# A state-space layer and a quantised feed-forward layer on eight cores: other buffers, queues and order for the weight preparation and the quantisation

## The chip, the cores and the metric

The kernel runs on one Trainium2 chip, on all 8 NeuronCores, with no exchange between them. Each core has a matrix engine (TensorE, PE in the profile), a vector engine (VectorE, DVE), an activation engine (ScalarE, ACT), a general engine (GpSimd, POOL) and a sync engine (SyncE, SP) that here only issues DMAs. The metric is the device time of the slowest core in microseconds (us); the kernel before takes 9439.07 us (median of 3 runs, 9436.37 to 9455.23).

## The reference

The input x is 2 sequences of 8192 tokens of 1024 features. Core c owns 2048 tokens of one sequence. What is computed, cut to its steps:

```python
# state-space half
xz = layernorm(layernorm(x)) @ W_in.T + b_in ; x_proj, z = split(xz) ; z = silu(z)
B_proj = x_proj @ W_B.T * dt.mean()
x_mean = causal convolution of B_proj with mean over d of A_bar[d] ** t
y = ((x_mean @ W_C.T + D_skip * x_proj) * z) @ W_out.T + b_out + residual
x = x + layernorm(y)
# feed-forward half (4096 hidden features)
def act_quant(x):    s = 127 / max|x| per token ; return clip(round(x * s), -128, 127) / s
def weight_quant(w): s = 1 / mean|w| ;            return clip(round(w * s), -1, 1) / s
h = act_quant(layernorm(x)) @ weight_quant(w1).T
h = silu(depthwise_conv1d(h, 3 taps) + conv_b)
x = x + layernorm(act_quant(h) @ weight_quant(w2).T)
```

## The kernel before

The program is written out by hand. `Pr` (from L49) keeps one list of instructions for each engine; an instruction is appended to its engine's list where the Python code calls it, with the semaphore values it has to wait for. So on each engine the order is that of the code, and an instruction that waits holds back all that is behind it on its engine. This is true of the DMAs too: `P.dma` appends the transfer to SP's list, or to POOL's with `eng="gpsimd"`. `P.bar()` gives the present value of every semaphore, and what waits for it waits for all work so far.

The stages of a core, one after the other:

1. A scan over the 6144 tokens ahead of its own, in three passes (L546). `range_pipeline` (L438) loads tiles of 128 tokens into `a_xtm`, transposes them and makes the sums for the layernorm.
2. Weight preparation (L618 to L650). Each of the 16 row blocks of W_in is loaded as 128x1024 (512 KB) into one of two halves of `a_big` (`natb`). For each of its 8 column blocks: PE transposes 128x128 into `ps0` or `ps1`, ACT writes the high bf16 part to `a_w1`, DVE writes the low part to `a_wr`, and a DMA stores this (32 KB) to `s_wlo` in DRAM. The next transpose waits for the store before it (`after=[lw] + wk[-2:]`, and a DMA's semaphore is waited for up to its latest value), so there are 128 such rounds. The 8 row blocks of W_out go the same way, without the store. Loads and stores are all on POOL's queue.
3. `range_pipeline` over the core's own tokens (L652, behind the barrier `ph4` ahead of stage 2), the projection (L683), the state-space part (L757 to L850).
4. The output projection in nine tiles of 256 tokens (L873), which ends with x2 in DRAM. Its tiles lie in `a_w1`'s memory, `a_st2`, `a_wr` and the last quarter of `a_big`.
5. `quant_weight` for w1 (L976): a first pass loads the 32 row blocks of w1 (SP's queue, two buffers in `a_xh`), ACT writes the absolute values to `a_xl`, DVE adds them up per row and into one column (three instructions one behind the other), then come the mean and its broadcast by way of DRAM; a second pass loads w1 again, rounds it to -1, 0, 1 and transposes it into `a_w1` and `a_w2`.
6. The feed-forward loop (L1130), 8 rounds `fi` of 256 tokens. The work of a round, in the order of the data:
   - x2 is loaded; squares (ACT) and column sums (PE); mean, maximum, scales, which go through rows in DRAM (`cols_to_row`, `bcast_read`);
   - the input is scaled and shifted: 16 POOL instructions of 128x258, four pairs ahead of the first `floor_sub` and four beside it (the list `uts2`), in `a_xh`. `floor_sub` (L255) is DVE's rounding, 17 instructions, and is called twice on 128x1032;
   - 32 hidden blocks of 128: 8 matmuls each, and DVE scales the sum from PSUM (`h_e`);
   - the convolution (ACT and DVE), silu (ACT), the maximum over the hidden features (DVE), scales, broadcast to `t_bt`;
   - the rounding of h, in 8 groups of 4 hidden blocks. For seven groups POOL multiplies (4 instructions of 128x256, two buffers in `a_xh`, function `emit_ug`) and DVE rounds: one instruction and a `floor_sub` of 128x1024. Group 7 is rounded by `floor_tri_act` (L280) in two halves: POOL multiplies (2 instructions), ACT does 18 absolute values of 128x512, DVE five instructions; the second half uses the same buffers and waits for the first. Each group is stored to `s_hq` from POOL's queue.

   This last step is put off by a round. `emit_hq_gps` (L1066), at the start of round fi+1, appends POOL's products for groups 0 and 1 and all of group 7; `emit_hq_vec` (L1095), behind the two input roundings of round fi+1, appends the DVE roundings of groups 0 to 6, the other products and the stores. After the last round both are called once more.
7. `quant_weight` for w2, and the output loop (L1310) of four tiles of 512 tokens, whose y tile changes between the two halves of `a_xl` (`yoff`).

## Time and profile before

| | |
|---|---|
| median of 3 timed runs | 9439.07 us |
| profiled execution, slowest core | 9412.07 us |
| span of that core (core 5) from first to last instruction | 9410.5 us |
| spans of the 8 cores | 9369.6 to 9410.5 us, granted clock 0.607 or 0.608 |
| PE, DVE, ACT, POOL busy in the span | 31%, 36%, 11%, 6% |
| DMA | 283.16 MB, mean 30 GB/s |
| chain that ended last, by what it spent time in | DVE 34%, PE 27%, DMA 15%, issue 11%, ACT 7%, POOL 1% |

Stage by stage, in us from the start of the span: scan 0 to 1693, weight preparation to 2381, own tokens, projection and state-space part to 3564, output projection to 4524, w1 to about 4970, feed-forward loop to 8332, w2 to about 8770, output to 9410. No engine is busy for even half of the span: in a program of this kind the time is a chain of waits from engine to engine, and a share of busy time says little. What counts is, in each stage, which instruction or transfer ends last before the next can start.

### The profile page before, as it was taken

What the parts mean: (1) busy time and instruction counts of PE and PEld (TensorE: products, weight loads), DVE (VectorE), ACT (ScalarE), POOL (GpSimd) and SP (SyncE); (2) the same over time, 40 slices, a digit from 0 to 9 for tenths busy, and PEclk for the clock granted to TensorE, in tenths of its full rate; (3) what the DMA queues carried; (4) which work ended last, traced back from release to release, by engine and by line L of the source; (5) the groups of instructions that cost most, each with busy time, mean ns of one, the idle gap of its engine ahead of it and who ended that gap; (6) DMA issues with size and microseconds to landing.
All of it is one profiled execution on the core that took longest, in us unless ns stands there. A gap on an engine that the chain in (4) does not pass through costs nothing.

```text
span 9410.5 us, 47615 instructions; the slowest of 8 cores (9369.6 to 9410.5 us)
## 1 busy us (share of the span) xinstructions
PE 2911.7 (31%) x12144; PEld 1440.0 (15%) x12144; DVE 3392.8 (36%) x6255; ACT 1064.5 (11%) x2053; POOL 520.5 (6%) x604
## 2 busy tenths in 40 slices
PE   3545354111557644333133010102101010103464
PEld 1121212000123343222011000101000000101121
DVE  0111110101112212333444575574757557564212
ACT  0111011001100020000101111202021120210000
POOL 0000000110000000000000111010111111000000
PEclk9955555555568856666556565656656565655686
DMA  1010101000001211111210000000000000021111
GB/s 32 26 41 32 42 27 38 28 23 25 31 32 40 37 39 26 32 36 32 90 45 17 8 9 8 14 10 11 9 8 9 8 14 10 3 98 54 42 56 59
DMA packets 170576, 283.16 MB, mean 30 GB/s; under 512 B 60305, under 2 KB 122987, under 8 KB 165893
## 3 DMA queue, kind: packets, MB, share of 16 engines
q1 hardware_dynamic: 157640, 246.56, 8.8%
q0 software_dynamic: 12672, 33.57, 1.2%
q8 instruction: 106, 1.74, 0.1%
q14 instruction: 158, 1.29, 0.0%
HBM read 223.21 MB, written 55.10 MB: 30 GB/s over the span
## 4 chain that ended last, share of the span: by engine, by line
DVE 34%; PE 27%; DMA 15%; issue 11%; ACT 7%; SPq 3%; DVEq 1%; POOL 1%; ACTq 0%; POOLq 0%
PE ps L243 21%; PE ps L246 6%; DVE a_xh_f L264 6%; DVE a_xh_f L260 5%; ACT a_st L272 4%; DMA a_st<-s_logat 3%; SPq L82 3%; DVE a_xh_f L252 3%; DMA s_wlo<-a_wr 2%; DVE a_st L264 2%; DMA s_rows<-t_tiny 2%; DVE a_w_f L252 2%; DVE a_w L249 2%; DVE a_xl_f L264 2%; DVE a_xtm L252 1%
## 5 line engine op out<-in xcount | busy, mean ns | idle before, releaser
L243 PE MATMUL ps<-a_xtm_b,a_w 128*128 128x258 bf16 x2048 | 295.8, 290 | 1548.1 <-DVE a_xh_f L252 1133.9
L264 DVE SCALAR_TENSOR_TENSOR a_xh_f<-a_xh_f 128x1024 f32<-128x1024 f32 x448 | 575.4, 1284 | 47.3 <-DVE a_xh_f L260 0.9
L243 PE MATMUL ps<-a_st,c_o1f 128*1 128x256 f32 (+3 forms) x992 | 415.0, 533 | 370.7 <-ACT a_st L272 323.8
L243 PE MATMUL ps<-a_xh,a_w 128*128 128x512 bf16 (+2 forms) x1664 | 386.1, 396 | 245.1 <-DMA a_xh<-s_hq 67.8
L246 PE MATMUL ps<-c_id,a_big 128*128 128x128 f32 x208 | 92.9, 447 | 1165.2 <-DVE a_big L252 532.4
L243 PEld LDWEIGHTS ps<-a_xtm_b,a_w 128*128 128x128 bf16 x2048 | 193.4, 102 | 1650.8 <-issue 1618.9
L246 PE MATMUL ps<-c_id,a_xh_f 128*128 128x128 f32 (+1 forms) x536 | 238.8, 445 | 658.9 <-DVE a_xh_f L252 392.3
L252 DVE TENSOR_TENSOR a_xl<-ps,a_xh 128x256 bf16<-128x256 f32 (+1 forms) x264 | 109.9, 416 | 857.5 <-ACT a_xh L272 857.5
L260 DVE TENSOR_SCALAR a_xh_f<-a_xh_f 128x1024 f32<-128x1024 f32 (+1 forms) x464 | 350.6, 756 | 144.3 <-POOL a_xh_f L252 95.2
L272 ACT ACTIVATE a_xl_f<-a_xh_f,c_cw 128x256 f32<-128x256 f32 x256 | 130.0, 508 | 1948.3 <-DVE a_xh_f L252 1948.3
L252 POOL TENSOR_TENSOR a_xh_f<-a_xl_f,t_bt 128x256 f32<-128x256 f32 x224 | 240.7, 1103 | 1950.4 <-DMA t_bt<-s_rows 1084.8
L243 PE MATMUL ps<-t_bt,a_st 128*128 128x16 f32 x1024 | 228.1, 373 | 322.9 <-ACT a_st L272 322.9
L249 DVE CAST a_w<-ps 128x128 bf16<-128x128 f32 x512 | 149.0, 291 | 359.3 <-PE ps L246 359.3
L243 PEld LDWEIGHTS ps<-t_bt,a_st 128*128 128x128 f32 x1024 | 223.1, 330 | 331.1 <-issue 331.1
L246 PE MATMUL ps<-c_id,a_xtm 128*128 128x128 f32 (+3 forms) x536 | 188.2, 441 | 244.8 <-DMA a_xtm<-xp 165.4
L243 PEld LDWEIGHTS ps<-a_xh,a_w 128*128 128x128 bf16 x1664 | 171.4, 105 | 459.3 <-issue 319.9
L264 DVE SCALAR_TENSOR_TENSOR a_xl_f<-a_xh_f,c_cw,a_xl_f 128x256 f32<-128x256 f32 x512 | 226.0, 481 | 27.1 <-DVE a_xl_f L264 0.5
L252 DVE TENSOR_TENSOR a_xh_f<-ps,a_xtm 128x258 f32<-128x258 f32 x256 | 109.0, 426 | 345.8 <-PE ps L243 345.8
L264 DVE SCALAR_TENSOR_TENSOR a_wr<-ps,c_vc,a_w 128x128 bf16<-128x128 f32 x128 | 44.8, 350 | 517.2 <-ACT a_w L272 517.2
L252 POOL TENSOR_TENSOR a_xh_f<-a_st,a_abc 128x258 f32<-128x258 f32 x64 | 54.4, 849 | 3175.4 <-DMA a_abc<-s_rows 3167.1
L246 PEld LDWEIGHTS ps<-c_id,a_big 128*128 128x128 f32 x208 | 37.9, 182 | 1220.0 <-issue 1220.0
L246 PEld LDWEIGHTS ps<-c_id,a_xh_f 128*128 128x128 f32 (+1 forms) x536 | 96.9, 181 | 800.4 <-issue 800.4
(189 smaller groups left out, 4883.0 us busy)
## 6 DMA issues: line engine op xcount, KB each, us to landing
a_st<-s_logat SPq DMA_DIRECT2D x64, 512.0 KB, 4.0
a_xh_f<-w SPq DMA_DIRECT2D x64, 512.0 KB, 3.8
a_xh_f<-w SPq DMA_DIRECT2D x16, 2048.0 KB, 8.2
a_xtm<-xp SPq DMA_DIRECT2D x48, 512.0 KB, 4.8
s_hq<-a_big_b POOLq DMA_DIRECT2D x64, 256.0 KB, 3.3
a_xh<-s_hq SPq DMA_DIRECT2D x128, 128.0 KB, 3.5
a_st<-s_x SPq DMA_DIRECT2D x64, 129.0 KB, 3.2
a_xtm<-xo SPq DMA_DIRECT2D x16, 512.0 KB, 4.7
```

The lines of the kernel that those rows point to most:

```text
L82: self.seq[eng].append((lambda e, o=out, i=in_: e.dma_start(out=o, in_=i), waits, (key, 16)))
L243: e.matmul(o, l, r, start=s1, stop=s2), after=after)
L246: return P.op(T, lambda e, o=out, i=in_, d=ident: e.transpose(o, i, d), after=after)
L249: return P.op(eng, lambda e, o=out, i=in_: e.tensor_copy(o, i), after=after)
L252: return P.op(eng, lambda e, o=out, x=a, y=b, p=op: e.tensor_tensor(o, x, y, op=p), after=after)
L260: e.tensor_scalar(o, x, u, w_, op0=p0, op1=p1), after=after)
L264: e.scalar_tensor_tensor(o, x, s, y, op0=p0, op1=p1), after=after)
L272: return P.op(eng, lambda e, o=out, i=in_, f=func, kw=kw: e.activation(o, i, f, **kw), after=after)
```

## The change

Four parts of the program change; every computed value stays.

1. **Weight preparation.** `natb` is `a_xtm`, not `a_big`; loads and stores go to SP's queue; the transposes use `ps5` and `ps6`; `wk` starts as one flat list, so that the first load waits for three tokens of the barrier (ACT, POOL, SP) and not for all. `range_pipeline` over the core's own tokens, whose buffer is the same `a_xtm`, waits for `ph1`, the barrier behind the weights.
2. **Sum of |w1|.** The first pass over w1 stands ahead of the output projection loop, with its loads on POOL's queue and its tiles in `a_big`. `quant_weight` for w1 gets the sum (`pre`) and starts with the mean. For w2 nothing changes.
3. **Feed-forward loop.** The rounding of h stands in its own round, behind the broadcast of the scales: groups 0 to 6, then group 7, then the stores. The input's eight pairs of POOL instructions all stand ahead of the first `floor_sub`, in `a_big`, and wait for the last stores from `a_big` (`prev_spill`).
4. **Output loop.** y stays in the first half of `a_xl`.

```diff
-    natb = [bigf[:, 0:1024], bigf[:, 1024:2048]]
-    wk = [list(ph4), list(ph4), list(ph4)]
+    natb = [sb_xtm.ap()[:, 0:1024], sb_xtm.ap()[:, 1024:2048]]
+    wk = list(ph4)
     for r in range(16):
         lw = P.dma(natb[r % 2], capd(d_win, r * 128 * D, [[1024, 128], [1, 1024]]),
-                   after=wk[-3:], eng="gpsimd", tag=f"wnat{r % 2}")
+                   after=wk[-3:])
         for k in range(KD):
-            bank = ps[0] if k % 2 == 0 else ps[1]
+            bank = ps[5] if k % 2 == 0 else ps[6]
...
-                       wrs, after=[lo], eng="gpsimd")
+                       wrs, after=[lo])
...
-    rp2 = range_pipeline(d_xo, 0, TLOC, ph4)
+    rp2 = range_pipeline(d_xo, 0, TLOC, ph1)
...
     ph5 = P.bar()
+    wmacc = []
+    wmpar = [list(ph5), list(ph5)]
+    for r in range(DH // 128):
+        pq_ = r % 2
+        lw = P.dma(bigf[:, pq_ * 1024:pq_ * 1024 + 1024],
+                   capd(d_w1, r * 128 * D, [[D, 128], [1, D]]),
+                   after=wmpar[pq_], eng="gpsimd", tag=f"wm{pq_}")
+        ab = act(bigf[:, 2048:3072], bigf[:, pq_ * 1024:pq_ * 1024 + 1024], AF.Abs,
+                 after=[lw] + wmacc[-1:])
+        rd = vred(colw[:, 126:127], bigf[:, 2048:3072], ALU.add, after=[ab])
+        wmpar[pq_] = [ab]
...
-        for r in range(kout):
...
+        else:
+            sm = mmo(ps[7].ap()[0:1, 0:1], sb_o1f.ap(), colw[:, 127:128], True, True,
+                     after=list(after) + pre)
...
     for fi in range(8):
         to = fi * 256
-        if pend_src is not None:
-            pend = ((pend_src[0],) + emit_hq_gps(pend_src[1], pend_src[2])
-                    + (pend_src[1], pend_src[2]))
...
-        for k in range(4):
-            usl = xhf[:, 2064 + k * 258:2064 + k * 258 + 258]
+        for k in range(KD):
+            usl = bigf[:, k * 258:k * 258 + 258]
             v1_ = vtt(usl, sb_st.ap()[:, k * 258:k * 258 + 258],
                       sb_abc.ap()[:, 0:258], ALU.mult,
-                      after=[bck] + uts[-1:], eng="gpsimd")
+                      after=[bck] + uts[-1:] + prev_spill, eng="gpsimd")
...
-        if pend is not None:
-            emit_hq_vec(*pend)
-            pend = None
         h_e = []
...
+        bk2 = bcast_read(sb_bt.ap()[:, 0:256], R_K2, to, 256, after=[rk2, rr2])
+        hq_fl = []
+        for gq in range(KH // 4):
+            if gq in ACTGQ:
+                continue
...
+                ug.append(vtt(xhf[:, uo + j * 256:uo + j * 256 + 256],
+                              xlf[:, mh * 256:mh * 256 + 256],
+                              sb_bt.ap()[:, 0:256], ALU.mult,
+                              after=[bk2] + hq_g[-1:] + hq_par[pa][-1:] + tr2[-1:],
+                              eng="gpsimd"))
...
+        for gq in ACTGQ:
...
+                    raws.append(vtt(xtmf[:, 1040 + j * 256:1040 + j * 256 + 256],
+                                    xlf[:, mh * 256:mh * 256 + 256],
+                                    sb_bt.ap()[:, 0:256], ALU.mult,
+                                    after=[bk2] + hq_act[-1:] + tr2[-1:],
+                                    eng="gpsimd"))
...
-            y5e.append(vtt(xlf[:, yoff + mo * 512:yoff + mo * 512 + 512],
...
+            y5e.append(vtt(xlf[:, mo * 512:mo * 512 + 512], ps[mo % 4].ap()[:, 0:512],
                            sb_abc.ap()[:, 0:512], ALU.mult,
-                           after=mms + [br2] + (tps_par[fj % 2] if mo == 0 else [])))
+                           after=mms + [br2] + (prev_tps[-1:] if mo == 0 else [])))
```

How instructions move, at the places that matter. First DVE where round fi's scales are done (the copies to `t_tiny`). Before, group 7's five instructions (`a_st`, `a_big_b`, 128x512) come twice, and then at once the copies of the sums of round fi+1 (1x258):

```order
L249 COPY t_tiny<-ps 2x128 x2
L257 TENSOR_SCALAR a_st<-a_st 128x512
L252 TENSOR_TENSOR a_st<-a_st 128x512
L257 TENSOR_SCALAR a_st<-a_st 128x512
L264 SCALAR_TENSOR_TENSOR a_st<-a_st 128x512
L264 SCALAR_TENSOR_TENSOR a_big_b<-a_xtm,a_st 128x512
L257 TENSOR_SCALAR a_st<-a_st 128x512
L252 TENSOR_TENSOR a_st<-a_st 128x512
L257 TENSOR_SCALAR a_st<-a_st 128x512
L264 SCALAR_TENSOR_TENSOR a_st<-a_st 128x512
L264 SCALAR_TENSOR_TENSOR a_big_b<-a_xtm,a_st 128x512
L249 COPY t_tiny<-ps 1x258 x2
```

Now the same place, where the seven groups of `a_xh_f` (128x1024) stand between; their last instruction is the first row:

```order
L264 SCALAR_TENSOR_TENSOR a_big_b<-a_xh_f 128x1024
L257 TENSOR_SCALAR a_st<-a_st 128x512
L252 TENSOR_TENSOR a_st<-a_st 128x512
L257 TENSOR_SCALAR a_st<-a_st 128x512
L264 SCALAR_TENSOR_TENSOR a_st<-a_st 128x512
L264 SCALAR_TENSOR_TENSOR a_big_b<-a_xtm,a_st 128x512
L257 TENSOR_SCALAR a_st<-a_st 128x512
L252 TENSOR_TENSOR a_st<-a_st 128x512
L257 TENSOR_SCALAR a_st<-a_st 128x512
L264 SCALAR_TENSOR_TENSOR a_st<-a_st 128x512
L264 SCALAR_TENSOR_TENSOR a_big_b<-a_xtm,a_st 128x512
L249 COPY t_tiny<-ps 1x258 x2
```

On DVE the 119 instructions of seven groups and their seven first ones have moved from behind the input rounding of the next round to ahead of group 7. The second place is POOL's list around a round. Before:

```order
L252 TENSOR_TENSOR a_xh_f<-a_st,a_abc 128x258
L252 TENSOR_TENSOR a_xh_f<-a_xh_f,a_bbc 128x258
L252 TENSOR_TENSOR a_xh_f<-a_xl_f,t_bt 128x256 x20
L82 DMA s_hq<-a_big_b 128x4x256 x8
L252 TENSOR_TENSOR a_xh_f<-a_xl_f,t_bt 128x256 x8
L252 TENSOR_TENSOR a_xtm<-a_xl_f,t_bt 128x256 x4
L252 TENSOR_TENSOR a_xh_f<-a_st,a_abc 128x258
```

And now (`a_big` in the first two rows is the input's new place):

```order
L252 TENSOR_TENSOR a_big<-a_st,a_abc 128x258
L252 TENSOR_TENSOR a_big<-a_big,a_bbc 128x258
L252 TENSOR_TENSOR a_xh_f<-a_xl_f,t_bt 128x256 x28
L252 TENSOR_TENSOR a_xtm<-a_xl_f,t_bt 128x256 x4
L82 DMA s_hq<-a_big_b 128x4x256 x8
L252 TENSOR_TENSOR a_big<-a_st,a_abc 128x258
```

Group 7's four products (`a_xtm`) stand behind all 28 of the other groups, and the stores behind both. The third place is SP's list at the weight preparation, where `a_st<-s_logat` are the last loads of the scan. Before:

```order
L82 DMA a_st<-s_logat 128x1x1024 x16
L82 DMA a_xtm<-xo 128x1024 x2
L82 DMA s_rows<-t_tiny 1x256 x2
L82 DMA a_xtm<-xo 128x1024 x2
L82 DMA s_rows<-t_tiny 1x256 x2
```

And now:

```order
L82 DMA a_st<-s_logat 128x1x1024 x16
L82 DMA a_xtm<-w_in 128x1024
L82 DMA s_wlo<-a_wr 128x128 x8
L82 DMA a_xtm<-w_in 128x1024
L82 DMA s_wlo<-a_wr 128x128 x8
```

All 24 loads and 128 stores of the weights have come from POOL's list to SP's, ahead of the loads of the core's own tokens.

## Rows read from the trace of the kernel before

**Rows 1.** Windows, two stages: PE, PEld, DVE, ACT, POOL busy, clock, DMA share, GB/s

```profile
4910.00:8340.00 3430.00, 441.73 (x2472) 242.15 (x2471) 2084.58 (x3223) 510.20 (x887) 438.30 (x448) 0.57 0.04 11
1693.00:2384.00 691.00, 88.51 (x200) 35.82 (x200) 63.91 (x193) 65.57 (x194) 81.98 (x152) 0.50 0.08 26
```

**Rows 2.** Timeline of POOL, input scaling: start us, us, engine and line, [idle before <-releaser]

```profile
5753.63 0.73 POOL L252 TENSOR_TENSOR a_xh_f<-a_st,a_abc 128x258 f32<-128x258 f32 x1 [69.30 <-DMA a_abc<-s_rows]
...
5770.06 1.45 POOL L252 TENSOR_TENSOR a_xh_f<-a_xh_f,a_bbc 128x258 f32<-128x258 f32 x1
```

**Rows 3.** Timeline of DVE, the two input roundings of the same round

```profile
5760.45 0.70 DVE L260 TENSOR_SCALAR a_xh_f<-a_xh_f 128x1032 f32<-128x1032 f32 x1 [11.77 <-POOL a_xh_f L252]
...
5781.34 0.70 DVE L260 TENSOR_SCALAR a_xh_f<-a_xh_f 128x1032 f32<-128x1032 f32 x1 [0.18 <-DVE a_xtm_b L264]
...
5798.47 1.23 DVE L264 SCALAR_TENSOR_TENSOR a_xtm_b<-a_xh_f,a_st 128x1032 bf16<-128x1032 f32 x1
```

**Rows 4.** Timeline of DVE, starts of groups 0, 1 and 2, and what follows group 6

```profile
5799.96 0.69 DVE L257 TENSOR_SCALAR a_xh_f<-a_xh_f 128x1024 f32<-128x1024 f32 x1
...
5818.92 0.69 DVE L257 TENSOR_SCALAR a_xh_f<-a_xh_f 128x1024 f32<-128x1024 f32 x1
...
5839.21 0.69 DVE L257 TENSOR_SCALAR a_xh_f<-a_xh_f 128x1024 f32<-128x1024 f32 x1
...
5939.64 0.42 DVE L252 TENSOR_TENSOR a_xh_f<-ps,a_xtm 128x258 f32<-128x258 f32 x1
```

**Rows 5.** Timeline of POOL and of PE in the same stretch

```profile
5839.50 4.90 POOL L252 TENSOR_TENSOR a_xh_f<-a_xl_f,t_bt 128x256 f32<-128x256 f32 x4 [15.39 <-DVE a_big_b L264]
...
5799.85 1.88 PE L243 MATMUL ps<-a_xtm_b,a_w 128*128 128x258 bf16 x8 [51.55 <-DVE a_xtm_b L264]
```

**Rows 6.** Timelines of POOL, ACT and DVE, from the scales' broadcast to the next squares

```profile
6072.05 5.67 POOL L252 TENSOR_TENSOR a_xh_f<-a_xl_f,t_bt 128x256 f32<-128x256 f32 x8 [130.30 <-DMA t_bt<-s_rows]
6077.68 1.40 POOL L252 TENSOR_TENSOR a_xtm<-a_xl_f,t_bt 128x256 f32<-128x256 f32 x2
6097.12 1.40 POOL L252 TENSOR_TENSOR a_xtm<-a_xl_f,t_bt 128x256 f32<-128x256 f32 x2 [18.04 <-DVE a_big_b L264]
...
6079.18 0.72 ACT L272 ACTIVATE a_st<-a_xtm,t_colw 128x512 f32<-128x512 f32 x1 [51.90 <-POOL a_xtm L252]
...
6098.61 0.72 ACT L272 ACTIVATE a_st<-a_xtm,t_colw 128x512 f32<-128x512 f32 x1 [5.09 <-POOL a_xtm L252]
...
6112.87 0.71 ACT L272 ACTIVATE a_st<-a_st 128x258 f32<-128x258 f32 x2
...
6093.62 0.43 DVE L257 TENSOR_SCALAR a_st<-a_st 128x512 f32<-128x512 f32 x1 [26.32 <-ACT a_st L272]
```

**Rows 7.** Timeline of DVE, its first instruction of the weight preparation

```profile
1699.77 0.35 DVE L264 SCALAR_TENSOR_TENSOR a_wr<-ps,c_vc,a_w 128x128 bf16<-128x128 f32 x1 [8.11 <-ACT a_w L272]
```

**Rows 8.** The chain of waits in the weight preparation: start us, us, what

```profile
1704.02 0.48 issue
1704.50 1.74 DMA s_wlo<-a_wr
...
1729.48 4.05 DMA a_big<-w_in
```

**Rows 9.** The chain of waits behind the first pass over w1 (SP's queue)

```profile
4619.22 1.09 DMA s_rows<-t_tiny
...
4624.32 3.84 DMA a_xh_f<-w
```

**Rows 10.** The tile s_x in stage 4: its 72 stores of 128 rows, SP's queue

```profile
DMA to landing us min/median/max: 1.6/2.7/5.2
```

**Rows 11.** Page, part 6: engine, count, KB each, median us from issue to landing

```profile
a_xtm<-xo SPq DMA_DIRECT2D x16, 512.0 KB, 4.7
```

**Rows 12.** Windows, the first pass over w1 (columns as in Rows 1)

```profile
4524.58:4617.70 93.12, 0.00 (x0) 0.01 (x1) 44.11 (x64) 33.79 (x32) 0.00 (x0) 0.50 0.58 180
```

**Rows 13.** Timeline of DVE at the start of the output projection loop

```profile
3575.78 0.42 DVE L252 TENSOR_TENSOR a_w_f<-a_w_f,a_st 128x256 f32<-128x256 f32 x1 [3.18 <-DMA a_st<-s_sz]
```

More of the change, by code:

```diff
@@ L637, in build_program @@
         lw = P.dma(natb[r % 2], capd(d_wout, r * 128 * D, [[1024, 128], [1, 1024]]),
-                   after=wk[-3:], eng="gpsimd", tag=f"wnat{r % 2}")
+                   after=wk[-3:])
         for k in range(KD):
-            bank = ps[0] if k % 2 == 0 else ps[1]
+            bank = ps[5] if k % 2 == 0 else ps[6]
             tp = tpose(bank.ap()[:, 128:256], natb[r % 2][:, k * 128:(k + 1) * 128],
@@ L854, in build_program @@
         P.dma(g["xmean"], sb_xm.ap(), after=ph5)
+    wmacc = []
[9 more added lines that the diff above has]
+        wmpar[pq_] = [ab]
+        if r == 0:
+            wmacc.append(vcopy(colw[:, 127:128], colw[:, 126:127], after=[rd]))
+        else:
+            wmacc.append(vtt(colw[:, 127:128], colw[:, 127:128], colw[:, 126:127],
+                             ALU.add, after=[rd]))
     def mv_cols(c0chunk, nt, after):
@@ L1049, in build_program @@
     ACTGQ = (7,)
-    prev_aspill, prev_dspill, last_raw = [], [], []
+    prev_aspill = []
     xtmf = sb_xtm.ap()
-    def emit_ug(gq, pa, hbk2, htr2l, extra):
-        uo = 4128 + pa * 1024
-        ug = []
-        for j in range(4):
-            mh = gq * 4 + j
-            ug.append(vtt(xhf[:, uo + j * 256:uo + j * 256 + 256],
-                          xlf[:, mh * 256:mh * 256 + 256],
-                          sb_bt.ap()[:, 0:256], ALU.mult,
-                          after=[hbk2] + hq_g[-1:] + extra + htr2l,
-                          eng="gpsimd"))
-        hq_g.append(ug[-1])
-        return uo, ug
@@ L1250, in build_program @@
             c1s.append(act(csl, xhf[:, mh * 258: mh * 258 + 256], AF.Copy,
-                           scale=sb_cw.ap()[:, mh * 3:mh * 3 + 1],
-                           after=[h_e[mh]]
-                           + (hq_g[-1:] + last_raw if mh == 0 else [])))
+                           scale=sb_cw.ap()[:, mh * 3:mh * 3 + 1], after=[h_e[mh]]))
         for mh in range(KH):
@@ new lines, in build_program @@
+        hq_fl = []
+        dvi = 0
+        for gq in range(KH // 4):
+            if gq in ACTGQ:
+                continue
+            pa = dvi % 2
+            dvi += 1
+            uo = 4128 + pa * 1024
+            ug = []
+            for j in range(4):
+                mh = gq * 4 + j
+                ug.append(vtt(xhf[:, uo + j * 256:uo + j * 256 + 256],
[3 more added lines that the diff above has]
+                              eng="gpsimd"))
+            hq_g.append(ug[-1])
+            w1b = vts(xhf[:, uo:uo + 1024], xhf[:, uo:uo + 1024],
+                      127.5, None, ALU.add, after=ug)
+            fl = floor_sub(bigb[:, gq * 1024:gq * 1024 + 1024],
+                           xhf[:, uo:uo + 1024],
+                           xhf[:, 6176:7200], xhf[:, 7200:8224], [w1b])
+            hq_par[pa] = [fl[-1]]
+            hq_fl.append((gq, fl[-1]))
@@ new lines, in build_program @@
+        for gq in ACTGQ:
+            fls = []
+            for hh in range(2):
+                raws = []
+                for j in range(2):
+                    mh = gq * 4 + hh * 2 + j
+                    raws.append(vtt(xtmf[:, 1040 + j * 256:1040 + j * 256 + 256],
[3 more added lines that the diff above has]
+                                    eng="gpsimd"))
+                hq_act = floor_tri_act(
+                    bigb[:, gq * 1024 + hh * 512:gq * 1024 + hh * 512 + 512],
+                    xtmf[:, 1040:1552],
+                    sb_st2.ap()[:, 1040:1552], sb_st2.ap()[:, 1552:2064], raws)
+                fls += hq_act
+            hq_fl.append((gq, fls[-1]))
@@ new lines, in build_program @@
+        for gq, ftok in hq_fl:
+            sp = P.dma(capd(s_hq, gq * 4 * 128 * TOWN + fi * 256,
+                            [[TOWN, 128], [128 * TOWN, 4], [1, 256]]),
+                       bigb[:, gq * 1024:gq * 1024 + 1024], after=[ftok],
+                       eng="gpsimd",
+                       tag=(f"hqa{gq % 2}" if gq in ACTGQ else f"hq{gq % 2}"))
+            if gq in ACTGQ:
+                prev_aspill = [sp]
+            else:
+                hq_d.append(sp)
+            hqs.append(sp)
@@ L1307, in build_program @@
+        prev_uts, prev_rr2 = uts[-1:], [rr2]
+        prev_he, prev_spill = h_e[-4:], hq_d[-2:]
     ph7 = P.bar()
```

181 lines of the change are left out of this document (54 added, 127 removed).

## The prediction, made before the changed kernel ran

> **What bounds the kernel now.** I read the page's table of engines first, then the windows by stage, then the timelines of single engines in the stages that the diff touches, and last the chain of waits for what lies between two engines. No engine is full. In the feed-forward stage DVE is busy 2085 of 3430 us and everything else far less [rows 1]; in the weight preparation no engine is busy for more than 13% of 691 us [rows 1]. So in each stage the question is what stands on the chain, and what DVE waits for.
>
> In the feed-forward loop one round takes 413.4 us. POOL scales the input; DVE starts its first input rounding 6.8 us after POOL's start [rows 2, 3] and needs 5799.70 - 5760.45 = 39.25 us for both roundings, of which the second, from 5781.34, takes 18.36 [rows 3]. The first takes 20.8 because POOL works beside it: POOL's last instruction starts at 5770.06 and takes 1.45, against 0.73 for the first [rows 2]. Then come the seven put-off groups: 5799.96 to 5939.64 = 139.7 us; a group takes 18.96 alone and 20.29 with POOL's four products beside it [rows 4]. POOL makes these products in 4.90 us and has then been idle for 15.39 us at each new group [rows 5]: DVE, not POOL, sets this pace. PE's first 8 matmuls (1.88 us) are under these groups [rows 5]. Then matmuls, convolution and maximum. From the landing of the scales the reader is to see a stretch in which DVE has nothing: POOL 5.67 + 1.40, ACT's 18 absolute values from 6079.18, DVE's five instructions from 6093.62, POOL again at 6097.12, ACT from 6098.61, and only at 6112.87 the squares of the next round. That is 6112.87 - 6072.05 = 40.8 us, with 3.5 us of DVE work in it [rows 6].
>
> **Feed-forward loop, the change.** The seven groups now stand on DVE directly behind the scales, ahead of group 7.
> - The start: POOL's four products for group 0 without DVE beside it, half of 5.67 = 2.8 us [rows 6], plus 0.1.
> - Seven groups. Group 1's products run beside group 0, group 6's beside group 5, so six groups take 20.3 and one 18.96; 0.4 for group 7's first two products: 141.1 us [rows 4, 5]. Two buffers are enough, since POOL has 15 us to spare.
> - Group 7, first half: its products are behind POOL's last four, thus at the start of group 5 plus 5 us; ACT needs 6093.5 - 6079.2 = 14.4 us [rows 6] and is done inside group 6. Hidden. On DVE its five instructions follow group 6: 3.5 us.
> - Group 7, second half, not hidden: POOL 1.5 with its hand-over, ACT 14.3 [rows 6]. DVE's last five are beside the squares, as now.
> Sum from the landing to the squares: 2.9 + 141.1 + 3.5 + 1.5 + 14.3 = 163.3. Before, the same work takes 40.8 + 139.7 = 180.5. Gain 17.2 a round; I take 16.9 for hand-overs, and eight times: -135.
> - Against it: all eight pairs of the input scaling are ahead of the first rounding. 6.8 us for the first four pairs; four more without DVE beside them +6.4 (8 instructions at 0.7 and 0.1 between). The first rounding is then as fast as the second, -2.4. Net +4.0 a round, +32.
> - PE's first 8 matmuls lose their cover: 1.88 + 0.3 less the 0.26 that DVE spent in between: +2.0, in seven rounds +14. Behind them is the same run of 31 blocks.
> - The stores wait on POOL behind group 7's products; seven of eight are issued under ACT's 14 us, and the next POOL work is 50 us away. The wait for `prev_spill` costs nothing; without that cover it would be a store's landing, some 3 us a round.
> Feed-forward loop: -135 + 32 + 14 = **-89 us**.
>
> **Weight preparation.** 128 rounds of transpose, ACT, DVE, store. In each, POOL begins the store 0.48 us after DVE and it lands after 1.74 [rows 8]. On SP's queue the hand-over is short: in the chain behind the w1 pass SP starts within 0.05 us. What a 32 KB store of 128 rows takes there no row shows. Nearest from below: a store of one row, 1.09 [rows 9]; from above: stores of 128 rows of 1 KB one behind the other, median 2.7, while the least of all (which has rows of 8 bytes in it) is 1.6 [rows 10]. I take 1.70, next to the 1.6, as the rows here have 256 bytes. Saved: 0.43 + 0.04 = 0.48 a round, 128 rounds: -61. The bounds are -61 - 128 x 0.61 = -139 and -61 + 128 x 1.0 = +67.
> - The Trainium skill ("DMA: Bandwidth & Descriptors", Latency and other measured facts) gives a first byte after about 1 us from GpSimd's queue and about 0.6 us from SP's. No row here shows the two for one transfer. By that, as an estimate, the store would land after some 1.35 us, and the gain of this term would be 45 us larger.
> - Loads of 512 KB: 0.52 + 4.05 on POOL [rows 8], 0.05 + 3.84 on SP [rows 9]; -0.7 for 15 + 8 loads: -17.
> - The first load no longer waits for DVE's scan. DVE idles 8.11 us ahead of its first instruction of this stage [rows 7]; this goes: -8.
> - The own tokens' first two loads had been made early and are now behind the barrier: 4.7 [rows 11] plus issue and start: +6.
> Weight preparation: -61 - 17 - 8 + 6 = **-80 us**.
>
> **Sum of |w1|.** The pass leaves its place: 93.1 us [rows 12], that is 3.84 for the first load and 32 x 2.79. It is not hidden in the new place, though: ACT and DVE take instructions in order, and the 32 absolute values and 64 DVE instructions stand ahead of the whole output projection loop. What is hidden is that loop's first loads: DVE can take its first product with the second load only at 3575.78, 12 us after the barrier at 3564 [rows 13]; with those loads under the pass, some 11.5 us go, less 0.6 for its own first instruction. The pass itself: first load 0.5 + 4.9, then two buffers whose cycle on POOL's queue is ACT 1.06 [rows 12] + 0.48 + 4.05 + 0.1 = 5.7 for two blocks, 2.85 each, a little more than 2.79: 5.4 + 31 x 2.85 + 2.5 = 96. Sum: -93 + 96 - 11 = **-8 us**, between -12 (pace still 2.79 and shorter first load) and +6 (loads of 4.9 us, as when two 512 KB loads are under way [rows 11], so 3.25 each).
> - By the same figures of the skill a load from POOL would be 0.4 us later than one from SP; the rows say 4.57 against 3.89, which is more, and the measured ones are in the sum.
>
> **Output loop.** The new wait is for transposes that stand on PE ahead of the matmuls whose sum is being read. It is over before it is asked for: 0.
>
> **Sum.** -89 - 80 - 8 = -177. The profiled execution took 9412; it would be 9235. The median of the runs is 27 us above it, so 9439 - 177 = **9262 us**.
>
> **Rivals.**
> A. The store on SP is like the 1 KB rows, 2.7 us: the weight term is +48 instead of -80, total -49, 9390. For it: the median in rows 10. Against: those stores have four times the bytes and came while DVE still fed them; the least is 1.6.
> B. Group 7's first half is not hidden, because its products are late on POOL: 14.4 us a round, +115, 9377. Against: POOL has 15 us idle in each group [rows 5].
> C. Slower. The groups now follow the scales at once, and each group's DVE work would have to wait for its products, if the two buffers gave no lead (a product waiting for the group before it and not the one before that). Place: the start of groups 1 to 6, 48 starts in all; price 4.96 us each, +238, 9500. It decides from 3.7 us a start (177 / 48). Against: the products wait for the buffer of two groups ago, and POOL's four are done 15 us before they are asked for.
> D. The put-off had a cover that I do not see (something on SP or PE that runs under the groups): about 10 us a round, +80, 9340.
>
> **Chances.** Forecast (all three terms within a fifth) 0.74; A 0.08; B 0.05; D 0.08; C 0.05. About 0.2%, 19 us, is what a measurement of this kernel can tell from no change; A, B and D are beyond it on the fast side. Faster 0.94, same 0.02, slower 0.04. The range: down to 9205 for the short store landing, up to 9345 for D and half of A.
>
> **What would show it.** The round of the loop at 402 to 403 us instead of 413.4. About 14 us between the second pair of group 7's products and the squares, and no ACT stretch of its own for the first half. DVE's first rounding at 18.4 us, 13 us after POOL's start. In the weight preparation, 3.3 us from store to store instead of 3.78. 32 blocks at 2.8 to 3.0 us ahead of the output projection, and its first matmuls behind them. The forecast is wrong if the groups' pace is above 20.5 us, if the store lands after 2 us or more, or if the time saved shows up again as a wait for the stores from `a_big`.

## Result, and the profile after

The changed kernel took 9218.39 us (median of 8 runs, 9195.31 to 9233.66) against 9436.37 for the kernel before (8 runs, 9426.14 to 9455.23): a ratio of 0.9768, 95% interval 0.9755 to 0.978, so 218 us less where 177 had been forecast. 9262 was predicted, 44 us too much and inside the range of 9205 to 9345.

All stage figures here are of core 7, which is the slowest core of the changed kernel's profile (span 9211.2 us), unless it says otherwise; of the kernel before core 7 is used too.

| stage | before | after | difference |
|---|---|---|---|
| end of the scan to the last weight tile | 691.6 | 567.0 | -124.6 |
| to the first projection (own tokens) | 317.5 | 327.9 | +10.4 |
| projections and state-space part | 849.8 | 875.8 | +26.0 (core 5: -12.5) |
| ahead of the output projection loop | 7.6 | 106.7 | +99.1 |
| output projection, sum of w1 where it was | 1048.8 | 957.3 | -91.5 (core 5: -102.6) |
| rest of w1 | 381.2 | 380.0 | -1.2 |
| feed-forward loop | 3333.7 | 3227.7 | -106.0 (core 5: -100.2) |
| w2 | 438.1 | 440.7 | +2.6 (core 5: -0.3) |

The third row is the same program in both kernels. Over the cores and kernels looked at (leaving out `e9_two_stores`, `v1_all` and `v2_all_w1`, which have a fault told of below) it lies between 848 and 904 us, which is more than some edits are worth. Three profiles show what goes with it, at the same instructions: 849.8 us with a DMA share (the mean busy share of the core's DMA engines) of 0.11 and a granted clock of 0.73 (before, core 7), 875.8 with 0.16 and 0.73 (changed kernel, core 7), 904.3 with 0.11 and 0.66 (`e3_w1sum`, core 5). What makes the transfers or the clock slower in one execution no run here shows. The whole span of core 7 is 188.5 us shorter, that of core 5 227.8, and the third row makes 38.5 of the 39.3 us between them; so single profiles are compared by stage, and small edits by their stage and by many runs.

First the two stages of [rows 1] in the changed kernel, same columns:

```profile
1688.00:2257.00 569.00, 85.23 (x191) 34.74 (x191) 63.57 (x193) 64.43 (x191) 0.00 (x0) 0.50 0.10 29
4903.00:8130.00 3227.00, 402.67 (x2408) 226.38 (x2408) 2039.44 (x3128) 510.27 (x887) 428.37 (x448) 0.58 0.04 10
```

The busy times of DVE and ACT are nearly what they were. POOL's 82 us in the weight preparation are gone, for they were the issuing of 152 DMAs, which SP now does; no engine has less arithmetic. What went is idle time. (The window of the feed-forward stage in [rows 1] begins some 90 us earlier and has the end of the w1 stage in it; over the loop alone, core 7, DVE is busy 2043 us before and 2040 after.) Next the chain of waits in the weight preparation, against [rows 8]:

```profile
1700.66 0.03 issue
1700.68 1.47 DMA s_wlo<-a_wr
...
1711.33 3.71 DMA a_xtm<-w_in
```

Hand-over and landing of a store are 1.50 us instead of 2.22, those of a load 3.74 instead of about 4.6. From one DVE instruction to the next it is 3.04 us, against 3.78. Of the 128 stores the median landing is 1.46 us on SP and 1.74 on POOL, on both cores looked at.

The feed-forward round, from the scaling on: POOL, then DVE (its two roundings start at 5777.00 and 5795.48), then PE. Start, us, what, and in brackets the idle time before:

```profile
5763.17 0.72 POOL L252 TENSOR_TENSOR a_big<-a_st,a_abc 128x258 f32<-128x258 f32 x1 [48.60 <-DMA a_abc<-s_rows]
...
5776.26 0.64 POOL L252 TENSOR_TENSOR a_big<-a_big,a_bbc 128x258 f32<-128x258 f32 x1
...
5777.00 0.70 DVE L260 TENSOR_SCALAR a_big<-a_big 128x1032 f32<-128x1032 f32 x1 [18.75 <-POOL a_big L252]
...
5795.48 0.70 DVE L260 TENSOR_SCALAR a_big<-a_big 128x1032 f32<-128x1032 f32 x1
...
5813.76 0.42 DVE L252 TENSOR_TENSOR a_xtm<-a_xtm 128x258 f32<-128x258 f32 x1
...
5813.99 1.88 PE L243 MATMUL ps<-a_xtm_b,a_w 128*128 128x258 bf16 x8 [56.13 <-DVE a_xtm_b L264]
5816.55 1.49 PE L243 MATMUL ps<-a_xtm_b,a_w 128*128 128x258 bf16 x8 [0.68 <-DVE a_xh_f L252]
```

The first rounding starts 13.8 us behind POOL's first instruction and takes 18.5 us. POOL keeps its 0.64 to 0.73 us to the end, where [rows 2] had 1.45. PE's first eight matmuls stand alone.

The same round from the landing of the scales on, POOL, ACT and DVE, against [rows 4 to 6]:

```profile
5947.75 8.07 POOL L252 TENSOR_TENSOR a_xh_f<-a_xl_f,t_bt 128x256 f32<-128x256 f32 x8 [170.86 <-DMA t_bt<-s_rows]
5971.22 4.90 POOL L252 TENSOR_TENSOR a_xh_f<-a_xl_f,t_bt 128x256 f32<-128x256 f32 x4 [15.39 <-DVE a_big_b L264]
5991.51 4.91 POOL L252 TENSOR_TENSOR a_xh_f<-a_xl_f,t_bt 128x256 f32<-128x256 f32 x4 [15.39 <-DVE a_big_b L264]
...
6057.27 2.86 POOL L252 TENSOR_TENSOR a_xtm<-a_xl_f,t_bt 128x256 f32<-128x256 f32 x2
6095.56 1.40 POOL L252 TENSOR_TENSOR a_xtm<-a_xl_f,t_bt 128x256 f32<-128x256 f32 x2 [35.43 <-DVE a_big_b L264]
6096.90 5.25 POOL L82 DMA_DIRECT2D s_hq<-a_big_b  x7
...
6060.22 0.72 ACT L272 ACTIVATE a_st<-a_xtm,t_colw 128x512 f32<-128x512 f32 x1 [157.15 <-POOL a_xtm L252]
...
6097.05 0.72 ACT L272 ACTIVATE a_st<-a_xtm,t_colw 128x512 f32<-128x512 f32 x1 [22.46 <-POOL a_xtm L252]
...
6111.30 0.71 ACT L272 ACTIVATE a_st<-a_st 128x258 f32<-128x258 f32 x2
...
6092.07 0.42 DVE L257 TENSOR_SCALAR a_st<-a_st 128x512 f32<-128x512 f32 x1
...
6121.60 0.41 DVE L249 COPY t_tiny<-ps 1x258 f32<-1x258 f32 x1 [6.75 <-PE ps L243]
```

ACT's first half (from 6060.22) lies under the groups, the second (6097.05) does not, and the next squares begin at 6111.30: 163.6 us behind the landing. The last row matters too: DVE, the engine with the most work, does nothing that is on the chain from 6095.4 to 6121.6 (group 7's last five instructions run beside the squares).

The last two places of the change: the own tokens behind the barrier (SP, ACT), and the |w1| pass at its new place (POOL, ACT, the third block):

```profile
2256.03 4.04 SPq L82 DMA_DIRECT2D a_xtm<-xo  x2
...
2264.24 0.38 ACT L272 ACTIVATE a_xh<-ps 128x256 bf16<-128x256 f32 x1 [9.52 <-PE ps L246]
...
3461.10 1.24 POOL L82 DMA_DIRECT2D a_big<-w  x2 [3460.40 <-issue]
...
3468.00 1.06 ACT L272 ACTIVATE a_big<-a_big 128x1024 f32<-128x1024 f32 x1 [23.48 <-DMA a_big<-w]
...
3476.21 1.06 ACT L272 ACTIVATE a_big<-a_big 128x1024 f32<-128x1024 f32 x1 [4.37 <-DMA a_big<-w]
```

Then the blocks follow at 2.8 to 3.3 us each.

### The profile page after: what moved, and what is told of

It is laid out like the page before. It is cut to its first block, busy times and chain, and to the rows that moved or that the text cites. A ratio compares the mean times of both kernels' runs of the same rounds, so it can differ in the third digit from the quotient of the medians.

```text
span 9211.2 us, 47621 instructions; the slowest of 8 cores (9147.2 to 9211.2 us)
## 1 busy us (share of the span) xinstructions
PE 2906.2 (32%) x12144; PEld 1437.3 (16%) x12144; DVE 3389.6 (37%) x6255; ACT 1064.5 (12%) x2053; POOL 445.7 (5%) x484
## 3 DMA queue, kind: packets, MB, share of 16 engines
q8 instruction: 106, 1.74, 0.1%
## 4 chain that ended last, share of the span: by engine, by line
DVE 34%; PE 28%; DMA 16%; issue 11%; ACT 6%; SPq 3%; DVEq 1%; POOL 1%; ACTq 0%; POOLq 0%
PE ps L243 21%; DVE a_xh_f L264 7%; PE ps L246 6%; DVE a_xh_f L260 4%; ACT a_st L272 3%; DMA a_st<-s_logat 3%; DVE a_xh_f L252 3%; SPq L82 2%; DMA s_rows<-t_tiny 2%; DVE a_w_f L252 2%; DVE a_st L264 2%; DMA s_wlo<-a_wr 2%; DVE a_w L249 2%; DVE a_xl_f L264 2%; DVE a_xtm L252 1%
## 5 line engine op out<-in xcount | busy, mean ns | idle before, releaser
L246 PE MATMUL ps<-c_id,a_xtm 128*128 128x128 f32 (+3 forms) x728 | 274.1, 442 | 758.2 <-DMA s_wlo<-a_wr 316.8
L243 PE MATMUL ps<-a_xh,a_w 128*128 128x512 bf16 (+2 forms) x1664 | 386.8, 396 | 247.0 <-DMA a_xh<-s_hq 68.1
L260 DVE TENSOR_SCALAR a_xh_f<-a_xh_f 128x1024 f32<-128x1024 f32 x448 | 345.5, 771 | 47.6
L252 POOL TENSOR_TENSOR a_xh_f<-a_xl_f,t_bt 128x256 f32<-128x256 f32 x224 | 259.5, 1187 | 1988.3 <-DMA t_bt<-s_rows 1371.5
L243 PEld LDWEIGHTS ps<-a_st,c_o1f 128*1 128x1 f32 x992 | 68.2, 85 | 1407.5 <-issue 1388.4
L246 PEld LDWEIGHTS ps<-c_id,a_xtm 128*128 128x128 f32 (+3 forms) x728 | 114.6, 195 | 1037.4 <-issue 1037.2
L264 DVE SCALAR_TENSOR_TENSOR a_w_f<-a_w_f,c_vc,ps 128x256 f32<-128x256 f32 (+1 forms) x144 | 65.0, 451 | 412.2 <-PE ps L243 410.7
L249 DVE COPY t_tiny<-ps 1x256 f32<-1x256 f32 (+8 forms) x201 | 71.0, 353 | 383.9 <-PE ps L243 182.0
```

The lines of the kernel that those rows point to most:

```text
L243: e.matmul(o, l, r, start=s1, stop=s2), after=after)
L246: return P.op(T, lambda e, o=out, i=in_, d=ident: e.transpose(o, i, d), after=after)
L249: return P.op(eng, lambda e, o=out, i=in_: e.tensor_copy(o, i), after=after)
L252: return P.op(eng, lambda e, o=out, x=a, y=b, p=op: e.tensor_tensor(o, x, y, op=p), after=after)
L260: e.tensor_scalar(o, x, u, w_, op0=p0, op1=p1), after=after)
L264: e.scalar_tensor_tensor(o, x, s, y, op0=p0, op1=p1), after=after)
```

## The experiments

Each ratio is against the kernel before, timed on the same chip, unless another is named.

**The four parts, one at a time.** `e1_weights` has the edit of the weight preparation (`natb`, queue, banks, `wk`, `ph1`), `e2_ffn` that of the feed-forward loop, `e3_w1sum` the moved sum of |w1| with `pre`, `e4_output` the output loop, each as in the diff of the change and nothing else.

> The kernel before with the weight preparation alone changed (stores and loads on SP's queue, buffers in a_xtm, banks 5 and 6, own tokens behind the barrier). Theory (the parts add up, each worth what its stage shows in the two traces): weight preparation 691 -> 567 us, 10 us back at the own tokens, thus 112 to 117 us less, 9320 to 9325 from 9437. Rival (the stage is shorter, but something later, such as the first loads of the output projection or the state-space part, takes part of it back unless the sum of |w1| is moved too): 60 to 100 us less.

> The kernel before with the feed-forward loop alone changed (groups behind the scales, all eight pairs of the scaling ahead). Theory (parts add up): round at 402 to 403 us against 414, 90 to 106 us less, 9331 to 9347. Rival (the loop gains from what stands ahead of it, the other queue or the moved sum): under 70 us less.

> The kernel before with the sum of |w1| alone moved ahead of the output projection. Theory (the traces of the whole change show +95.5 to +99 there and -93 where it was, and the first loads of the projection under it -1): between 10 us less and 8 us more, no difference that can be told. Rival (it was worth what the two other parts don't explain, or its price there came only with the other parts): more than 20 us less.

> The kernel before with the output loop alone changed (one y buffer instead of two). Theory: the wait for the transposes is over before it is asked for, 0 within 5 us. Rival (the next 512 columns had worked ahead on DVE under the last transposes, three times): 10 to 30 us more.

| kernel | us | ratio, 95% interval | its stage |
|---|---|---|---|
| e1_weights | 9310.59 | 0.9875 [0.9852, 0.9898] | 564.6 + 328.3, as in the whole change |
| e2_ffn | 9333.16 | 0.9891 [0.9872, 0.991] | 3230.9 |
| e3_w1sum | 9425.63 | 0.9999 [0.9979, 1.0019] | 106.9 and 943.5 |
| e4_output | 9448.42 | 1.0007 [0.9992, 1.0022] | - |

The kernel before, timed beside them, took 9432.44 us (23 runs). The parts are thus -122, -99, and twice nothing that can be told (-7 and +16 by the medians, within the intervals); the first two together -221 +- some 30, all four -212, against the -218 measured for the whole. They add up, and two of them carry everything. The interval of `e4_output`, up to 1.0022 or 21 us, does not by itself exclude its rival of 10 to 30 us more. The trace does: the output loop, from its first load of `s_hq` to the end, takes 636.4 and 641.8 us on cores 5 and 7, against 637.4 and 642.2 before.

**What of the weight preparation does it.** `e5_queue_only` is the kernel before with the following edits (the first one stands twice, for w_in and for w_out)

```diff
-                   after=wk[-3:], eng="gpsimd", tag=f"wnat{r % 2}")
+                   after=wk[-3:], tag=f"wnat{r % 2}")
...
-                       wrs, after=[lo], eng="gpsimd")
+                       wrs, after=[lo])
```

and `e6_stores_only` has the second of these edits alone.

> The kernel before with the queue alone changed: all stores and loads of the weight preparation on SP; buffers, banks and the barrier for the own tokens as before. Theory (the queue carries the gain: landing plus hand-over 2.22 -> 1.54 us, period 3.78 -> 3.03): weight preparation at 563 to 572 us, 9310 to 9325. Rival (banks 5 and 6, or buffers outside a_big, free the start of each round): under half of it, 9370 or more.

> The kernel before with the 128 stores alone on SP, the loads left on POOL. Theory (a hand-over and a landing for each instruction, added up): stores 128 x 0.75 = 96 us less in the weight preparation, the loads' 23 x 0.9 = 20 us missing against the run with both. Rival (one queue has to hold both, since a wait between two queues costs what it saves): 60 us less or under.

Measured: 9328.27 us, 0.9862 [0.9842, 0.9882], and 9351.59 us, 0.9892 [0.9871, 0.9912]; from its first to its last DVE instruction the stage takes 568.3 and 583.9 us, against 681.8 before and 566.7 in the changed kernel. The queue does it, though 9328 is 3 us above the 9310 to 9325 expected. The rest of the edit cancels out: the first load that waits for three tokens of the barrier takes away the wait ahead of the first tile (from the start of the scan's last DVE instruction to the first tile 8.3 and 9.6 us before, 5.5 in `e5_queue_only`, 0.1 in the changed kernel), and the barrier for the own tokens, which the buffer in `a_xtm` makes necessary, costs 10: their stage is 317.8 us in `e5_queue_only`, against 327.9. The chain of `e6_stores_only` has both prices side by side, the store on SP, the load on POOL:

```profile
1725.13 1.46 DMA s_wlo<-a_wr
1726.63 0.54 issue
1727.16 4.21 DMA a_big<-w_in
```

By the stage, 98 us for the stores and 16 for the loads: 128 x 0.75 = 96 and 23 x 0.9 = 20 were expected.

**The input scaling.** `e7_scaling` is the changed kernel with

```diff
-                        bigf[:, 2064:3096], sb_st2.ap()[:, 0:1032], uts)
+                        bigf[:, 2064:3096], sb_st2.ap()[:, 0:1032], uts[:4])
...
-                        bigf[:, 2064:3096], sb_st2.ap()[:, 0:1032], fla[-1:])
+                        bigf[:, 2064:3096], sb_st2.ap()[:, 0:1032],
+                        uts[4:] + fla[-1:])
```

> The changed kernel with one wait given back: the first input rounding waits for the first four pairs of POOL's scaling, the second for the other four (all in a_big as now). Theory (the scaling ahead of the rounding cost 4.0 us a round, 7.0 for the longer scaling less 2.4 to 3.0 for DVE without POOL beside it): first rounding 6.8 us behind POOL's start and 20.8 long, 8 x 4.0 to 4.6 = 32 to 37 us less, 9182 to 9187 from 9218. Rival (the separate buffers in a_xh made that lead possible, or the late scaling was free): 0.

9204.01 us, 0.9738 [0.9723, 0.9752]: 14 us less than the changed kernel by the medians; 28 less by the ratios 0.9738 and 0.9768, each against the kernel before timed beside it (9447.41 us here, 9436.37 beside the changed kernel); and by the stage 3203.9 instead of 3227.7 us, 24 less (core 5: 28). The rows of POOL and DVE side by side:

```profile
5366.22 0.64 POOL L252 TENSOR_TENSOR a_big<-a_big,a_bbc 128x258 f32<-128x258 f32 x1
5367.00 1.25 POOL L252 TENSOR_TENSOR a_big<-a_st,a_abc 128x258 f32<-128x258 f32 x1
5368.39 1.53 POOL L252 TENSOR_TENSOR a_big<-a_big,a_bbc 128x258 f32<-128x258 f32 x1
...
5366.96 0.70 DVE L260 TENSOR_SCALAR a_big<-a_big 128x1032 f32<-128x1032 f32 x1 [12.14 <-POOL a_big L252]
...
5369.44 1.03 DVE L260 TENSOR_SCALAR a_big<-a_st 128x1032 f32<-128x1032 f32 x1
...
5387.85 0.70 DVE L260 TENSOR_SCALAR a_big<-a_big 128x1032 f32<-128x1032 f32 x1 [0.18 <-DVE a_xtm_b L264]
```

The start moves from 13.8 to 7.1 us behind POOL's, the first rounding takes 20.9 instead of 18.5: 4.3 us a round on this piece, as forecast (4.0). Of these, 3.3 (core 7) and 3.9 (core 5) arrive in each of the six rounds in the middle, which take 399.0 and 398.7 us instead of 402.2 and 402.6. Up to the scaling of the second round the stage gains under 1 us; why not more there I have not found. The theory's 32 to 37 us was too much, the rival's 0 is refuted.

**Group 7 among the others.** `e8_group7_early` is the changed kernel with the products and the rounding of group 7 moved into the loop over the groups:

```diff
+            if gq in (1, 3):
+                raws = []
...
+                    mh = 28 + (gq // 2) * 2 + j
...
+            if gq in (2, 4):
+                hh = gq // 2 - 1
+                hq_act = floor_tri_act(
...
-        for gq in ACTGQ:
```

> The changed kernel with group 7's work placed among the others: its two pairs of products on POOL behind those of groups 1 and 3, ACT's values beside groups 2 and 4, DVE's five instructions behind groups 2 and 4. Theory (what stands on the chain at the round's end is ACT's second half alone, and it also holds up the next squares in ACT's order): from the end of the last group to the next DVE copy of the sums, 29.5 us now, nearly nothing is left but 3.3 us more for DVE; 23 us a round in seven rounds and 17 in the last, 9035 to 9050. Rival (the next round's squares wait for something else, such as the stores or the loads of x2; then only ACT's half goes): 12 to 16 us a round, 9090 to 9120. Other rival (ACT beside the groups slows DVE): pace of a group above 21 us, the gain under 100 us.

9080.38 us, 0.9609 [0.9593, 0.9625]: 138 us less than the changed kernel by the medians, 150 by the ratios; the stage takes 3085.6 instead of 3227.7 us (core 5: 3077.2 instead of 3232.4). POOL, ACT, DVE:

```profile
5921.23 8.07 POOL L252 TENSOR_TENSOR a_xh_f<-a_xl_f,t_bt 128x256 f32<-128x256 f32 x8 [173.29 <-DMA t_bt<-s_rows]
...
5989.19 2.20 POOL L252 TENSOR_TENSOR a_xtm<-a_xl_f,t_bt 128x256 f32<-128x256 f32 x2 [18.59 <-DVE a_big_b L264]
...
5991.48 0.72 ACT L272 ACTIVATE a_st<-a_xtm,t_colw 128x512 f32<-128x512 f32 x1 [44.85 <-POOL a_xtm L252]
...
6005.79 0.71 ACT L272 ACTIVATE a_st<-a_st 128x258 f32<-128x258 f32 x2
...
5647.34 1.03 DVE L252 TENSOR_TENSOR a_st<-a_st 128x512 f32<-128x512 f32 x1
...
5688.46 1.23 DVE L264 SCALAR_TENSOR_TENSOR a_big_b<-a_xh_f 128x1024 bf16<-128x1024 f32 x1
5689.60 0.41 DVE L249 COPY t_tiny<-ps 1x258 f32<-1x258 f32 x1
```

The next round's squares (6005.79) are made under the groups, and DVE's copy of the sums stands directly behind the last group (5689.60, one round earlier). This is the theory's mechanism. The size is a little less. From the landing of the scales (5921.23 in this round) to DVE's copy of the sums it is 151.8 or 151.9 us in every round, against 172.2 to 173.8 in the changed kernel: 21 us instead of the 23 expected, which had counted all of DVE's ten instructions for group 7. Part of the rest is that two of the groups now share their time with six products of POOL and take 21.0 us instead of 20.3, and that some of the ten instructions stand beside products too (the tensor-tensor 1.03 us instead of 0.69). A round in the middle is 19.3 us (core 7) and 20.0 (core 5) shorter. Both rivals fall: a round gained more than 12 to 16 us, and the pace of a group is 20.3 to 21.0 us with a gain of over 100.

**The chain of the weight preparation cut.** `e9_two_stores`, on the changed kernel:

```diff
-                       sb_id.ap(), after=[lw] + wk[-2:])
+                       sb_id.ap(), after=[lw] + (los[-2:-1] or ph4))
...
-                      ALU.mult, ALU.subtract, after=[hi])
+                      ALU.mult, ALU.subtract, after=[hi] + sps[-2:-1])
...
-                       wrs, after=[lo])
+                       wrs, after=[lo], tag=f"wlo{k % 2}")
```

and each 512 KB load issued ahead of the tiles of the block before it, with a name for each of the two buffers.

> The changed kernel with the chain of the weight preparation cut: a transpose waits for its bank alone (the DVE instruction two tiles ago), DVE for the store of two tiles ago instead of PE for the last store, and the next 512 KB are loaded under the transposes of the ones before. Theory (SP's queue is idle nearly all of the 3.03 us; what the move to it saved was latency on a chain, not work): store cycle 0.35 + 0.07 + 1.47 + 0.1 = 2.0 us for two tiles, 1.0 each; 128 x 1.0 + 64 x 0.8 + 5 = 185 us instead of 566, 8840 from 9218. Rival (two stores under way take 2.7 us each, as the 1 KB rows in the trace of before do, or SP issues one at a time): 128 x 1.6 to 1.9 + 51 = 255 to 295 us, 8910 to 8950.

9130.4 us, 0.9675 [0.9641, 0.9709]: only 88 us less than the changed kernel, where theory and rival both wanted 270 or more. Yet the stage itself did nearly what was expected, 205.2 us from its first to its last DVE instruction (185 had been the theory's figure, 255 to 295 the rival's), as DVE shows with two tiles in about 2.0 us:

```profile
1743.28 0.78 DVE L264 SCALAR_TENSOR_TENSOR a_wr<-ps,c_vc,a_w 128x128 bf16<-128x128 f32 x2 [1.48 <-DMA s_wlo<-a_wr]
...
1745.32 0.82 DVE L264 SCALAR_TENSOR_TENSOR a_wr<-ps,c_vc,a_w 128x128 bf16<-128x128 f32 x2 [1.27 <-DMA s_wlo<-a_wr]
```

From the scan's end to the last tile the stage takes 210.9 us instead of 566.9, 356 less. This gain has two parts that no run separates: the stores that no longer wait for one another, and the 23 loads that are now under the tiles. At 3.74 us each (hand-over and landing in the changed kernel) the loads are, as an estimate, 86 us of it. Of the 356 us some 245 came back in the two stages behind, which no edit had touched: 13 at the own tokens (341.0 instead of 327.9) and 232 in the projections (1107.3 instead of 875.8). There:

```profile
2445.37 9.85 PE L243 MATMUL ps<-a_xh,a_w 128*128 128x410 bf16 x40 [27.40 <-DMA a_wr<-s_wlo]
...
2479.69 15.77 SPq L82 DMA_DIRECT2D a_wr<-s_wlo  x8
```

against, in the changed kernel, an idle time of 10.1 us and 4.8 us of issuing:

```profile
2787.36 10.04 PE L243 MATMUL ps<-a_xh,a_w 128*128 128x410 bf16 x40 [10.05 <-DVE a_big L257]
...
2787.71 4.81 SPq L82 DMA_DIRECT2D a_wr<-s_wlo  x8
```

Eight small loads one after the other. The cause, which `v3_own_names` below shows, is in how this program writes waits down: a DMA's token is resolved to the newest count of its name when the waiting instruction is added (`v = self.cnt[s]` in `_flat`). I had given the stores the names `wlo0` and `wlo1`, which the loads of the projections have too. So the barrier `ph2` contained them, and each load and each first matmul that waits for `ph2` now waited for the newest load.

**The gains in one kernel, with that fault and without.** `v1_all` has `e7_scaling`, `e8_group7_early` and `e9_two_stores`, with buffers, banks and the own tokens' early loads as before the change. `v2_all_w1` has in addition the 32 blocks of the |w1| pass in the weight preparation, two for each 128 rows of w_in, loads on POOL's queue into `a_xh`. `v3_own_names` differs from `v2_all_w1` in one line, `tag=f"wls{k % 2}"`.

> What the runs so far point to, in one kernel: the changed kernel with the cut chain of the weight preparation, its buffers and banks and the own tokens' early loads as before the change, group 7 among the others, and the first rounding behind four pairs of the scaling. If the gains add up: (changed) 9218 - (cut chain) 270 to 380 - 10 - 138 - 14 to 26 = 8665 to 8785. If they get in each other's way, over 8800.

> The same with the pass for the sum of |w1| inside the weight preparation: its 32 loads on POOL's queue, two blocks under the tiles of each 128 rows of w_in. Theory (ACT and DVE are idle for over half of a tile there; the pass costs 105 us where it stands): ACT 1.06 and DVE 1.2 us for each block, the loads 16 MB more in a stretch of 130 us, which at the pass's own 0.5 MB in 2.79 us would want 90 to 120 us with the rest; 60 to 90 us less than the kernel beside it. Rival (the pass is bound by memory wherever it stands, since all eight cores load): under 30 us.

> The last kernel with one thing changed: its two semaphores for the stores of the weight preparation have names of their own. In the runs with the cut chain the projections took 50 us a tile instead of 34, 1107 to 1120 us for the stage instead of 850 to 876: the trace shows the eight loads a_wr<-s_wlo one after the other (15.8 us of issuing instead of 4.8) and PE 27.4 us idle ahead of each tile, with the last of them as the releaser. Theory (a wait on a DMA is resolved to the newest count of its name when it is written down; the stores carried the names that the loads of the projections use, so the barrier ahead of the stage now meant each newest load): with names of their own the stage is back at 850 to 880 us, 230 to 260 us less, 8615 to 8645. Rival (the shorter weight preparation leaves the PE clock lower or the memory slower in the next stage): no change, 8875.

The column of the weights is from the stage's first to its last DVE instruction.

| kernel | us | ratio, 95% interval | weights | projections, state space | feed-forward |
|---|---|---|---|---|---|
| v1_all | 8929.55 | 0.9463 [0.9432, 0.9495] | 203.6 | 1119.7 | 3047.4 |
| v2_all_w1 | 8875.12 | 0.9406 [0.9382, 0.9431] | 246.3 | 1110.4 | 3044.1 |
| v3_own_names | 8610.36 | 0.9118 [0.9097, 0.9139] | 247.0 | 851.2 | 3046.8 |

`v1_all` missed its 8665 to 8785 because of the names. The |w1| pass costs 43 us inside the weight preparation and 95 to 99 where it stood: 52 to 56 by the stages and 54 by the medians, just short of the 60 to 90 expected; the rival of under 30 falls. No instruction of this stretch is seen to wait for a block of |w1|. What is seen is that the transfers beside them land later: the 512 KB loads of w_in after 5.2 to 5.4 us in the median instead of 4.0, and some stores after up to 5.2 us instead of 3.9, for which DVE waits:

```profile
1855.90 0.61 DVE L264 SCALAR_TENSOR_TENSOR a_wr<-ps,c_vc,a_w 128x128 bf16<-128x128 f32 x2 [4.50 <-DMA s_wlo<-a_wr]
```

The new names gave 265 us back, slightly more than the 230 to 260 expected: 259 in the projections, with 34 us a tile again, and 14 at the own tokens (319.0 instead of 332.9), which the expectation had left out. This settles the cause; the rival, a lower clock or slower memory behind the short stage, falls. (The granted clock of the slow projections of `e9_two_stores` was 0.68 instead of 0.73, but PE was busy for 539 us there and 549 in the changed kernel: it waited.) The rows:

```profile
2332.85 9.91 PE L243 MATMUL ps<-a_xh,a_w 128*128 128x410 bf16 x40 [10.06 <-DVE a_big L257]
2333.19 4.83 SPq L82 DMA_DIRECT2D a_wr<-s_wlo  x8
```

`v3_own_names` is 8.8% faster than the kernel before, and 608 us faster than the changed one.

## Why the prediction was right, and where it was off

- **The forecast as a whole.** The time is inside the range, but the case that the chances called the forecast, all three terms within a fifth, did not come about: the loop's term is 12 to 19% larger, the weight term 43%, and the third cannot be told from zero. The first two erred to the same side, so the 44 us are their errors added up and not errors that cancelled. Of the signs that were named, the round (402.2 and 402.6 us), the first rounding (18.5 us, 13.8 behind POOL's start) and ACT's one open stretch came as said; the distance from store to store was to be 3.3 us and was 3.04.
- **Feed-forward loop, -89 forecast, -100 to -106 measured.** The sum from the landing to the squares came out at 163.6 us (163.3 forecast), the pace of a group at 20.3. Scaling and first matmuls cost 4.6 and about 2 us (+4.0 and +2.0). A round is 11.5 us shorter on average over the six in the middle (10.9 forecast). The rest is at the two ends: on core 5 the stretches before the second round's scaling and behind the last one's lost 31 us together, where two average rounds would have lost 23. I had not looked at the ends apart.
- **Weight preparation, -80 forecast, -114 measured.** The mechanism was right, one term was mis-sized: "I take 1.70" for the landing of a 32 KB store on SP. It took 1.47, and with the hand-over a tile lost 0.74 instead of 0.48 us: 128 x 0.27 = 34 us, which is as much as the whole miss. By the Trainium skill ("DMA: Bandwidth & Descriptors", Latency and other measured facts) the estimate had been 1.35 us and 45 us more gain; the trace, with 1.47, lies nearer to that than to my value. For the same store it has 1.74 on POOL and 1.47 on SP, a difference of 0.27 us where the page's figures give 0.4. The loads (16 for 17 us) and the first load (8 to 10 for 8) are nearly as forecast; the own tokens cost 10.4 instead of 6, since the two loads came behind each other and the first ACT instruction needs both.
- **Sum of |w1|, -8 forecast; nothing that could be measured.** `e3_w1sum` alone gives 0.9999. The two traces of the whole change give +7.6 and -7. The first block was used, by the rows in the result, 6.9 us after its issue (4.9 assumed, where [rows 11] had 4.7), beside the output projection's own first loads; whether these loads are hidden under the pass, the two traces show only within the scatter of the cores.
- **Output loop, 0 forecast; 1.0007,** and the loop's own time is the same to 1 us (see `e4_output`). Right.
- **The rivals.** A (a store like the 1 KB rows): 1.47 us. B (first half of group 7 late): it lies under group 5 and 6. C (groups wait for their products): POOL is idle for 15.39 us ahead of each. D (a cover I don't see): the loop gave more than forecast, not less.
- **What the prediction did not ask.** It took the put-off of the groups as a question of 17 us a round. `e8_group7_early` shows that the change leaves another 21 at the same place, and `e9_two_stores` that the 3 us store chain need not be a chain at all.

## What to carry to other kernels

Where no engine is full, ask of each stage which chain it runs on, and try first to cut the chain (a second buffer and a wait for the turn before the last) and only then to shorten its links by another queue: here the queue gave 114 us of the 682 between the first and the last DVE instruction, the cut together with the loads ahead 362 of the remaining 567. Whether the queue still matters once the chain is cut no run here shows. When a stage gets faster and the next one slower without an edit to it, compare the waits of that stage by releaser before blaming the chip; one semaphore's name used in two places was worth 265 us here. Put the work of a side engine early in the sequence of the busy one, so that its last part is not what the next round waits for.
